# First feed-forward: pipeline order, a third butterfly level on VectorE, and ternary weights by a Sign on ScalarE

## The reference, cut to what matters

```python
def act_quant(x, bits=8):
    qb = float(2 ** (bits - 1))
    scale = qb / jnp.clip(jnp.max(jnp.abs(x), axis=-1, keepdims=True), EPS)
    return jnp.clip(jnp.round(x * scale), -qb, qb - 1) / scale

def weight_quant(w):
    scale = 1.0 / jnp.clip(jnp.mean(jnp.abs(w)), EPS)
    return jnp.clip(jnp.round(w * scale), -1.0, 1.0) / scale

gate = act_quant(x) @ weight_quant(w_gate).T       # 256 -> 1024
up = act_quant(x) @ weight_quant(w_up).T
inter = silu(gate) * up
y = act_quant(fwht(inter)) @ weight_quant(w_down).T  # 1024 -> 256
```

## Time and profile before

| | us |
|---|---|
| median of 3 runs | 1540.13 |
| lowest, highest | 1536.32, 1545.28 |
| the profiled execution, its own time | 1544.92 |
| its span, first to last instruction | 1543.1 |

### The profile page before, as it was taken

One profiled execution on the slowest core, in us unless ns is written; L12 is line 12 of the kernel. 1 busy time (PEld: TensorE's weight loads), 2 busy tenths in 40 slices (PEclk: granted clock), 3 DMA queues, 4 the chain that ended last, 5 costly groups with the idle time before them and its releaser, 6 DMA issues.

```text
span 1543.1 us, 23269 instructions
## 1 busy us (share of the span) xinstructions
PE 1224.4 (79%) x8532; PEld 868.8 (56%) x8577; DVE 873.9 (57%) x1827; ACT 607.1 (39%) x1322; POOL 345.1 (22%) x264
## 2 busy tenths in 40 slices
PE   1572476489888369869999982999997899999986
PEld 1352254244343336558888871556555688888854
DVE  6678754566777456244454457333335676665576
ACT  2432232055556223124333321333333475565443
POOL 1327000111110100012211201544541142222313
PEclk9655698588899579989999985999997999999998
DMA  7100000700000321230000031111103000000010
GB/s 246 37 2 1 0 1 1 309 12 1 1 1 1 120 74 65 88 129 1 1 1 1 1 110 67 52 52 51 41 10 115 1 1 1 1 1 1 1 42 27
DMA packets 32306, 64.44 MB, mean 42 GB/s; under 512 B 5360, under 2 KB 23280, under 8 KB 30288
## 3 DMA queue, kind: packets, MB, share of 16 engines
q1 hardware_dynamic: 31440, 61.03, 11.2%
q0 software_dynamic: 768, 2.10, 0.4%
HBM read 55.39 MB, written 9.70 MB: 42 GB/s over the span
## 4 chain that ended last, share of the span: by engine, by line
PE 51%; issue 18%; DVE 12%; POOL 3%; ACT 3%; DMA 2%; DVEq 0%; SPq 0%; POOLq 0%; ACTq 0%
PE psum L1398 8%; PE psum L1380 4%; PE psum L2417 4%; PE psum L2445 4%; PE psum L2407 3%; PE psum L736 2%; PE psum L2389 2%; PE psum L2371 2%; PE psum L1040 2%; PE psum L1066 2%; PE psum L2743 1%; PE psum L1008 1%; POOL a_q_rstd L2262 1%; PE psum L1073 1%; PE psum L2034 1%
## 5 line engine op out<-in xcount | busy, mean ns | idle before, releaser
L1465 DVE TENSOR_TENSOR m_silu_up<-psum,m_silu 128x512 f32<-128x512 f32 x50 | 34.6, 692 | 132.6 <-PE psum L1398 132.6
L1132 ACT ACTIVATE c_probs<-psum 128x512 f32<-128x512 f32 x128 | 76.3, 599 | 68.8 <-PE psum L1051 68.8
L1236 DVE TENSOR_REDUCE c_max<-psum 128x2 f32<-128x512 f32 x128 | 84.6, 687 | 32.6 <-PE psum L1040 25.8
L1398 PE MATMUL psum<-ctxT_yT_hi,m_w_lo 128*128 128x512 bf16 x200 | 76.5, 382 | 8.5 <-DVEq L1457 7.2
L1398 PE MATMUL psum<-ctxT_yT_lo,m_w_hi 128*128 128x512 bf16 x200 | 76.3, 382 | 0.0
L1493 POOL TENSOR_TENSOR m_h_lo<-m_h,m_h_hi 128x512 bf16<-128x512 f32 x50 | 57.8, 1157 | 82.0 <-ACT m_h_hi L1437 82.0
L2445 PE MATMUL psum<-a_wo,a_outT 128*128 128x256 f32 x256 | 75.1, 405 | 0.7 <-DVE x_tok L2626 0.7
L2062 PE MATMUL psum<-a_wo,a_outT 128*128 128x256 f32 x256 | 75.2, 407 | 0.0
L1249 POOL TENSOR_TENSOR c_rope_terms<-c_rope_terms 128x256 f32<-128x256 f32 x16 | 11.6, 725 | 281.3 <-DVE c_rope_terms L1192 281.3
L1437 ACT ACTIVATE m_h_hi<-m_h 128x512 bf16<-128x512 f32 x50 | 31.5, 629 | 91.2 <-DVE m_h L1470 91.2
L1398 PE MATMUL psum<-ctxT_yT_hi,m_w_hi 128*128 128x512 bf16 x175 | 66.8, 382 | 0.0
(11 more groups left out here) (480 smaller groups left out, 3554.0 us busy)
## 6 DMA issues: line engine op xcount, KB each, us to landing
m_w<-m_w SPq DMA_DIRECT2D x8, 1536.0 KB, 16.5
m_w<-m_w SPq DMA_DIRECT2D x27, 384.0 KB, 3.0
a_wq<-a_wq SPq DMA_DIRECT2D x2, 2048.0 KB
a_wo<-a_wo SPq DMA_DIRECT2D x2, 2048.0 KB, 12.3
a_trig<-trig_sin_cos SPq DMA_DIRECT2D x1, 2048.0 KB, 6.2
ctxT_yT_hi<-f_gate_up SPq DMA_DIRECT2D x2, 1024.0 KB, 6.6
a_sin_cos<-a_trig SPq DMA_DIRECT2D x1, 2048.0 KB, 10.1
m_rows<-m_zeros SPq DMA_DIRECT2D x1, 1920.0 KB, 14.1
```

The source lines that it names most:

```text
L1132: e.activation(c1P[:, n % 8, :, :], ps[:, 2 + n % 2, :].rearrange("p (k t) -> p k t", k=2), ACT.Exp, scale=float(1.0 / np.sqrt(np.float32( ...
L1236: e.tensor_reduce(c1M[:, u % 2, j, :], ps[:, c1_score_bank(n), :].rearrange("p (q t) -> p q t", q=2), AX.X, ALU.max).then_inc(c1_mx, 1)
L1398: ins = e.matmul(ps[:, bank, :], l[:, s, o + kc * P:o + (kc + 1) * P], r[:, kc, tk], start=(x == 0), stop=(x == 3 * KC - 1))
```

## The change

In stage 2 GpSimd no longer clips. `f0_ternary` applies Sign instead of Identity to the rounded weights less the large number, waits for `f0_scaled` alone, and stands elsewhere in ScalarE's queue: the first behind the squares of i = 5 and the second behind those of i = 6, both ahead of the last exponential.

In stage 3 VectorE does a third butterfly level into a new buffer `f0C`, and the Hadamard product has 128 columns per matmul. The down product goes to bank 0, and waits for the Silu of the tile after next to have been taken from there. The order within a step is new on all three engines. ScalarE calls Silu once on one value at the head of its program.

```diff
             def f0_ternary(n):
-                e.wait_ge(f0_qd, n + 1)
-                e.activation(f0q[:, n, :], f0w[:, n, :], ACT.Identity, bias=f0c[:, 11:12]).then_inc(f0_q, 1)
+                e.wait_ge(f0_r, 4 + n)
+                e.activation(f0q[:, n, :], f0w[:, n, :], ACT.Sign, bias=f0c[:, 11:12]).then_inc(f0_q, 1)
...
-                if i >= 6:
-                    f0_ternary(i - 6)
                 if i >= 3 and i % 2:
                     squares(i // 2 - 1)
+                if 5 <= i < 7:
+                    f0_ternary(i - 5)
...
-            def f0_clipped(n):
-                e.wait_ge(f0_r, 4 + n)
-                e.tensor_scalar(f0w[:, n, :], f0w[:, n, :], ROUND - 1.0, ROUND + 1.0, ALU.max, ALU.min).then_inc(f0_qd, 1)
...
-                if u == 1:
-                    f0_clipped(0)
-                    f0_clipped(1)
-            f0_clipped(2)
...
             def gate_or_up(i, r):
                 if i:
                     e.wait_ge((f0_si, f0_us)[r], i)
+                if r == 0 and i >= 4:
+                    e.wait_ge(f0_ou, i - 3)
...
             def inter_turned(i):
                 e.wait_ge(f0_bf, i + 1)
+                if i:
+                    e.wait_ge(f0_te, i)
                 if i >= 2:
                     e.wait_ge(f0_zt, i - 1)
-                    e.wait_ge(f0_ou, i - 1)
...
             def hadamard(i):
...
                 for j in range(FJ):
-                    c = j // 2 * 2 * P
-                    ins = e.matmul(ps[:, 4 + c // 512, c % 512:c % 512 + 2 * P], f0T[:, i % 2, j, :], f0hd[:, (j % 2) * P:(j % 2 + 2) * P],
-                                   start=(j % 2 == 0), stop=(j % 2 == 1), skip_group_check=True)
+                    ins = e.matmul(ps[:, 4 + j // 4, (j % 4) * P:(j % 4 + 1) * P], f0T[:, i % 2, j, :], f0hd[:, :], start=True, stop=True)
...
             def down(i):
...
                 e.wait_ge(f0_zt, i + 1)
+                e.wait_ge(f0_si, min(i + 4, NT))
+                if i:
+                    e.wait_ge(f0_ou, i)
                 for j in range(FJ):
-                    ins = e.matmul(ps[:, 7, 0:D], f0zT[:, i % 2, j, :], f0q[:, 2, j * D:(j + 1) * D], start=(j == 0), stop=(j == FJ - 1))
+                    ins = e.matmul(ps[:, 0, 0:D], f0zT[:, i % 2, j, :], f0q[:, 2, j * D:(j + 1) * D], start=(j == 0), stop=(j == FJ - 1))
...
             for n in F0_STEPS:
+                if f0_tile(n, 2) is not None:
+                    z_turned(n - 2)
                 if f0_tile(n, -1) is not None:
                     gate_or_up(n + 1, 0)
                     gate_or_up(n + 1, 1)
-                if f0_tile(n, 1) is not None:
-                    hadamard(n - 1)
+                if f0_tile(n, 0) is not None:
+                    inter_turned(n)
                 if f0_tile(n, 2) is not None:
-                    z_turned(n - 2)
                     down(n - 2)
                 if f0_tile(n, 0) is not None:
-                    inter_turned(n)
+                    hadamard(n)
...
         def f0_act(e):
+            e.activation(f0c[:, 15:16], f0c[:, 10:11], ACT.Silu)
...
             for n in F0_STEPS:
                 if f0_tile(n, 2) is not None:
-                    rounded(n - 2)
+                    zT(n - 2)
                 if f0_tile(n, -1) is not None:
                     silu(n + 1)
-                if f0_tile(n, 2) is not None:
-                    zT(n - 2)
+                if f0_tile(n, 1) is not None:
+                    rounded(n - 1)
                 if f0_tile(n, 0) is not None:
                     interT(n)
...
             def butterflies(i):
                 e.wait_ge(f0_us, i + 1)
+                if i >= 2:
+                    e.wait_ge(f0_tp, i - 1)
...
+                e.tensor_tensor(w[:, :, 0, :], v[:, :, 0, :], v[:, :, 1, :], ALU.add)
+                dve_step(e, e.tensor_tensor(w[:, :, 1, :], v[:, :, 0, :], v[:, :, 1, :], ALU.subtract))
+                v, w = (t.rearrange("p (a two c) -> p a two c", a=4, two=2) for t in (u, f0C[:, i % 2, :]))
...
             for n in F0_STEPS:
-                if f0_tile(n, 0) is not None:
-                    inter(n)
-                if f0_tile(n, 2) is not None:
-                    z_int(n - 2)
-                if f0_tile(n, 0) is not None:
-                    butterflies(n)
+                if f0_tile(n, 1) is not None:
+                    z_scale(n - 1)
+                if f0_tile(n, -1) is not None:
+                    inter(n + 1)
+                if f0_tile(n, 1) is not None:
+                    z_int(n - 1)
                 if f0_tile(n, 2) is not None:
                     residual(n - 2)
-                if f0_tile(n, 1) is not None:
-                    z_scale(n - 1)
+                if f0_tile(n, -1) is not None:
+                    butterflies(n + 1)
```

More of the change, by code:

```diff
@@ L661, in program @@
         f0B = m("f0_inter_halfway", [P, FF0], F32)
+        f0C = m("f0_inter_butterflied", [P, 2, FF0], F32)
         f0T = m("f0_interT", [P, 2, FJ, P], F32)
@@ L666, in program @@
         f0k = m("f0_token_factors", [P, 3, NT], F32)
-        f0hd = sb("f0_hadamard", [P, 3 * P])
+        f0hd = sb("f0_hadamard", [P, P])
         f0c = sb("f0_scalars", [P, 32])
@@ L722, in inter_turned @@
                 e.wait_ge(f0_bf, i + 1)
+                if i:
+                    e.wait_ge(f0_te, i)
                 if i >= 2:
                     e.wait_ge(f0_zt, i - 1)
-                    e.wait_ge(f0_ou, i - 1)
                 for j in range(FJ):
-                    ins = e.transpose(ps[:, 6 + j // 4, (j % 4) * P:(j % 4 + 1) * P], f0A[:, i % 2, j * P:(j + 1) * P], identf[:, :])
+                    ins = e.transpose(ps[:, 6 + j // 4, (j % 4) * P:(j % 4 + 1) * P], f0C[:, i % 2, j * P:(j + 1) * P], identf[:, :])
                 ins.then_inc(f0_tp, 1)
@@ L758, in f0_pe @@
                     gate_or_up(n + 1, 1)
-                if f0_tile(n, 1) is not None:
-                    hadamard(n - 1)
+                if f0_tile(n, 0) is not None:
+                    inter_turned(n)
                 if f0_tile(n, 2) is not None:
-                    z_turned(n - 2)
                     down(n - 2)
                 if f0_tile(n, 0) is not None:
-                    inter_turned(n)
-            finish(e, 3, e.matmul(ps[:, 0, 0:1], identb[:, :], identb[:, 0:1], start=True, stop=True))
+                    hadamard(n)
+            finish(e, 3, e.matmul(ps[:, 7, 0:1], identb[:, :], identb[:, 0:1], start=True, stop=True))
         def f0_act(e):
+            e.activation(f0c[:, 15:16], f0c[:, 10:11], ACT.Silu)
             for cc in range(KC):
@@ L869, in residual @@
                 e.wait_ge(f0_o, i + 1)
-                e.scalar_tensor_tensor(xt[:, i, :], ps[:, 7, 0:D], f0m[:, 16 + i:17 + i], xt[:, i, :], ALU.mult, ALU.add).then_inc(f0_ou, 1)
+                e.scalar_tensor_tensor(xt[:, i, :], ps[:, 0, 0:D], f0m[:, 16 + i:17 + i], xt[:, i, :], ALU.mult, ALU.add).then_inc(f0_ou, 1)
             for n in F0_STEPS:
-                if f0_tile(n, 0) is not None:
-                    inter(n)
-                if f0_tile(n, 2) is not None:
-                    z_int(n - 2)
-                if f0_tile(n, 0) is not None:
-                    butterflies(n)
+                if f0_tile(n, 1) is not None:
[4 more added lines that the diff above has]
+                    z_int(n - 1)
                 if f0_tile(n, 2) is not None:
                     residual(n - 2)
-                if f0_tile(n, 1) is not None:
-                    z_scale(n - 1)
+                if f0_tile(n, -1) is not None:
+                    butterflies(n + 1)
             e.wait_ge(f0_ou, NT)
@@ L2889, in constants @@
         h = np.block([[h, h], [h, -h]])
-    c["hadamard"] = np.concatenate([h, h, -h], 1)
+    c["hadamard"] = h
     d = p % 8
```

1 line of the change is left out of this document (removed).

## The result

The changed kernel takes 1494.55 us, median of 4 runs (1493.52 to 1499.09), against 1538.22 for the kernel before, measured beside it in 4 runs (1536.09 to 1545.28): a ratio of 0.971, 95% interval 0.968 to 0.975, or 43.7 us less. The profiled executions differ by 45.8 us, 1544.92 against 1499.09 own time. The forecast was 1500. The page's chain of work that ended last, for the earlier trace rows, has TensorE at 50% where it had 51, and VectorE at 14% where it had 12.

The account below looks back on a forecast made before the run. The prediction took VectorE, held by GpSimd clips, to bound the attention's end, and a round trip through TensorE to bound the feed-forward loop. Gains 16.1 + 23.5 = 39.6 us off 1540.1 gave 1500.5, written 1500; range 1491 to 1513.

Parts of the forecast that it names:

- Stage A: Last third of the recurrent attention: three VectorE instructions freed from GpSimd clips, 14.7 us, plus 1.4 us less waiting: 16.1 us gained.
- ScalarE's queue with table loads for Sign: Rival, attention: Sign outside Exp's table set, each switch costing 2.57 us, last exponential 4.2 us late: 1505 us; chance 0.08.
- About 3.0 us of waiting per tile before: Old feed-forward loop: TensorE spends about 3.0 us per tile waiting for ScalarE's copy of z and for the residual.
- Period 8.21 with VectorE as bound: New feed-forward loop: VectorE's work per tile sums to 8.21 us and sets the period, against 10.95 us before.
- The Hadamard product: Feed-forward loop: 128 columns instead of 256 shorten the product from 3.45 us to about 1.73, estimated by halving.
- The third rival, no shrinking: Feed-forward loop: Hadamard instructions keep their length because each also loads weights: 1503 us; counted within the forecast's 0.70.
- The first two tiles: Start of the feed-forward loop: first gate matmul at 174.37, inter and butterflies of tiles 0 and 1 done at 188.0.
- The last tile: End of the feed-forward loop: rounding, copy and Hadamard product 6.1 us plus 1.8 for low clock; after last integer z 5.31.
- What the saving is counted from: Whole kernel: 39.6 us subtracted from the runs' median, 1540.1, since the profiled execution lay 4.8 us above it.
- stage B: The feed-forward loop, profile times 174 to 277: new order and third butterfly level end it at 253.3 against 276.8, 23.5 us gained.
- "Later stages are not touched": Everything after the feed-forward loop: assumed unchanged, so nothing was added to or taken from the forecast for it.
- The rival of the low clock: Feed-forward loop: TensorE at 1.2 GHz adds 3.0 us per tile; all tiles 1519 us, chance 0.06; about half 1509, part 0.12.

Follow-up runs that it names:

- clips_unused: The changed kernel with two GpSimd clips of 128x2048 put back on already ternary weights, nothing waiting for them and their result unused: 1519.10 us, ratio 0.985.
- act_queue: The kernel before, clips kept on GpSimd, with all three Identity passes moved to the end of ScalarE's queue: 1540.41 us, ratio 1.000.
- a_alone: The kernel before with only the attention part of the change (Sign, no clips, new places in ScalarE's queue), feed-forward loop as before: 1520.24 us, ratio 0.987.
- zint_act: The changed kernel with the integer z made by ScalarE instead of VectorE, without the upper limit of 127: 1494.82 us, ratio 0.970.
- level_alone: The kernel before with only the third butterfly level and the 128-column Hadamard product, old order and old attention: 1538.22 us, ratio 0.998.

## Why the prediction was right, step by step

The forecast of 1500 held: 1494.55 at first, 1506.96 and 1501.60 when measured again. Against the kernel before beside each, that is 43.7, 33.3 and 39.5 us less, where 39.6 had been forecast. What bears the prediction is the working of the two stages, below; that the whole time comes so near to 1500 is in part luck, since it wanders by 12 us.

- **Stage A, 16.1 forecast.** The stage begins 0.8 us earlier by itself and ends (L602) at 137.53 instead of 154.51: 16.98 - 0.77 = 16.2. The three long rows gave 6.29, 4.29 and 4.17, the power wait 1.47. Both parts are shown separately, by clips_unused (10.7 for the first two) and act_queue (1.4). The third long row, 4.86 us, only came and went with the third clip (act_queue, a_alone). Sign cost 1.99. The prediction finds VectorE nearly without gaps in stage A; that is so from 118 us on, but further ahead it waits 3.44 and 2.91 us for TensorE's scores, before and after alike (3.43 and 2.92).
- **ScalarE's queue with table loads for Sign (0.08).** It did not come: no load was made for L483. The Trainium skill (ScalarE: Activation LUTs, What ACT_TABLE_LOAD costs) charges 2.66 us for a switch to another set; the Signs of stage A caused no switch, so this has nothing to apply to. The trace before could have ruled the rival out. What the prediction says for it, that Sign occurs nowhere in that trace, is wrong: L1741 is a Sign, in layer 1's feed-forward, and comes behind an exponential (L1743), a Copy and an Abs with no load in between. The load behind it is for Silu (L1756).

```profile
524.50 0.21 ACT L1743 ACTIVATE m_prob<-m_max 128x8 f32<-128x8 f32 x1 [9.61 <-DVEq L1776]
...
528.48 1.91 ACT L1741 ACTIVATE ctxT_yT_lo<-ctxT_yT_lo 128x2048 bf16<-128x2048 bf16 x1
530.41 1.28 ACT L1756 ACT_TABLE_LOAD   x1
```

- **Silu's load at zero.** Right, it lies at 131.71 under VectorE's work.
- **About 3.0 us of waiting per tile before.** The size is right and its parts are not: the prediction names the wait for the copied z and that for the residual, which are 1.12 and 0.67 us. The other 1.25 is the wait for `inter` shown above, which the new order removes as well.
- **Period 8.21 with VectorE as bound.** It was 8.12, and zint_act shows that VectorE is what sets it. The 0.09 is mostly the butterflies, 204.07 - 200.21 = 3.86 and not 3.93. Counted from the start of a scale, the integer z was due at 3.26 us and came at 3.27, and the Hadamard product at 4.2 and came at 4.12.
- **The Hadamard product.** Halving was off by a tenth: from its start to that of the next instruction 201.96 - 200.07 = 1.89 us, not 1.73 (232.13 - 230.34 = 1.79 in level_alone). That did not matter, since the product ends at 202.12, 1.95 us before the scale takes it at 204.07. The third rival, no shrinking, was wrong.
- **The first two tiles, 13.6 forecast from the first gate to the first scale.** 14.3: the first Hadamard product took 3.48 us at the lower clock and VectorE waited 0.60.
- **The last tile.** Forecast 7.9 to its scale, 7.1 measured; its end 5.31 forecast, 4.05 measured. The last turning and down product ran at full clock (0.62 and 1.05 us where the earlier trace rows's stretch had 1.03 and 1.89). The loop gave 24.7 where 23.5 was forecast; the errors are +0.7 in the first two tiles, +0.2 in the middle ones, -0.8 and -1.3 here.
- **What the saving is counted from.** The prediction takes 39.6 us off the median of the runs, but had read the old loop's end, 276.8, in a profiled execution 4.8 us above that median. In this profile the last two Hadamard products ran slowly; against the loop of a_alone, 101.9 us instead of 106.9, the saving of stage B would have been some 5 us less. Which course the unprofiled runs took is not known.
- **"Later stages are not touched"** is a step that did not hold in the numbers. Of the 45.8 us between the profiles, 16.2 + 24.8 are the two stages. Another 0.8 lies ahead of stage A, whose start differs among all these profiles, 65.9 to 68.6 us, and 4.1 us stand in the attention of layer 1, 224.9 against 220.8. It has the same 1524 matmuls in both:

```profile
276.82:501.60 224.78, 181.54 (x1524) 84.62 (x1524) 154.09 (x336) 112.38 (x231) 28.65 (x48) 0.82 0.14 56
```

```profile
235.04:455.60 220.56, 177.41 (x1524) 83.28 (x1524) 155.19 (x341) 112.06 (x231) 28.66 (x48) 0.83 0.14 57
```

TensorE was 4.1 us less busy for the same instructions. Of the four kernels with the old order three show 224.9 to 225.9 there and one, a_alone, 220.6; the eight profiles with the new order show 218.0 to 223.6. Whether a kernel that comes there earlier takes the shorter course more often, or this is chance, stays open; it would take many profiles of both.

The rival of the low clock came in a small form: it appeared in the first, third, sixth and last Hadamard products (3.48, 2.70, 3.39 and 2.94 us) and cost 0.60, 0.33 and 0.36 us, plus part of the last wait, not the 3.0 us per tile that the prediction gives a clock low throughout. The 0.79 of the second window is one of the signs that the prediction had named against itself, a granted clock well below 1.00 in the middle of the loop; it was there, and cost a third of a microsecond. The 11.2 us of TensorE time from which the 3.0 follow are twice 5.6, the starts from one instruction to the next; by the busy 6.2 us they would be 12.4. No run had the low clock throughout, so neither is shown.

## What to carry to other kernels

Here the long GpSimd clips, which cost only 1.4 us by being waited for, held up VectorE for 14.8 us, in rows that are short elsewhere (4.86 us for 0.69): look for twins of one line with different lengths before looking at waits. In a loop where no engine is full, write down the round trip with every wait in it, and then reorder so that each wait has another tile's work in it. Once one engine shows no waits, take work off that engine, as zint_act did. A change worth 9 us in a stage can vanish in the whole time when later stages wander by as much, as level_alone's did, so measure the stage. And before giving a chance to what an instruction might do, search the old kernel for one of its kind.

## What the runs showed of the hardware

- A 128x32 tensor_scalar on VectorE took 6.47 us under a GpSimd tensor_scalar of 128x2048 and 0.38 to 1.75 under memsets, where it takes 0.18 alone; a 128x32 tensor_tensor took 4.47 under the first and 0.18 under the second. The tensor_scalar ended with the clip, the tensor_tensor 2.5 us before the clip did.
- Sign next to Exp, Square and Identity on ScalarE loaded no table (106.38 to 116.60 us in the changed kernel).
- An untouched stretch of 93.5 us took 98.9 in other executions of the same program, at a granted clock of 0.53 instead of 0.87 over 20 us. The same program measured three times gave ratios of 0.971, 0.974 and 0.980, and the last lies outside the 95% interval of the first (0.968 to 0.975): an interval from runs of one session doesn't hold what differs from one session to the next.
- 16 float32 Hadamard matmuls at full clock took a row of 2.05 us with 128 columns and of 3.62 with 256: a little more than half.
